# Five row buffers, three sets of statistics and four places for transposes in the first routing of a Macaron block

## The reference

```
x = x + 0.5 * switch_ffn(layernorm(x))     # 8 experts of 1024 hidden units, capacity 512 tokens each
x = x + attention(layernorm(x))            # 16 heads of 16, RMS norm and rotary on q and k
x = x + 0.5 * switch_ffn(layernorm(x))     # the same weights again

# inside switch_ffn, for the 8192 tokens in order:
probs = softmax(x @ w_switch + b_switch);  routes = argmax(probs)
pos   = cumsum(onehot(routes)) * onehot - 1          # place in the expert's queue
keep  = pos < 512;  slot = routes*512 + pos          # those beyond the capacity pass unchanged
y     = relu(buf[slot] @ w1 + b1) @ w2 + b2
```

## Time and profile before

| | |
|---|---|
| median of 3 executions | 2530.02 us (2524.09, 2530.02, 2530.95) |
| profiled execution, its own time | 2523.72 us |
| its span, first to last instruction | 2521.9 us |
| TensorE, busy share of the span | 87% |
| VectorE, ScalarE | 69%, 69% |
| GpSimd | 39% |
| last scatter of the first routing landed | 192.75 us |
| first expert matmul (L619) | 202.92 us |

### The profile page before, as it was taken

How to read it: one execution, slowest core, us unless ns; L and a number is a source line. 1 busy time by engine, 2 the same in 40 slices (tenths; PEclk the granted TensorE clock), 3 DMA queues, 4 the chain that set the end, 5 groups by cost and what they waited for, 6 DMA issues and landing times.

```text
span 2521.9 us, 36418 instructions
## 1 busy us (share of the span) xinstructions
PE 2198.5 (87%) x12974; PEld 1157.5 (46%) x12974; DVE 1738.2 (69%) x2555; ACT 1739.2 (69%) x3390; POOL 977.4 (39%) x1157
## 2 busy tenths in 40 slices
PE   3648994279999989999999998999999999964997
PEld 3547883234434434443443443444344334223986
DVE  2535673467888788887888878888777988302774
ACT  3655666216788778878878877887887887733663
POOL 2554532164056247326515723722651101112542
PEclk9999997658999999999999999999999999755999
DMA  6522530503523334324533332542343422103331
GB/s 244 169 81 101 176 135 25 125 8 85 90 56 86 76 74 86 92 50 86 115 69 83 81 77 57 91 98 56 73 102 61 81 44 32 49 9 126 117 135 59
DMA packets 144901, 218.29 MB, mean 87 GB/s; under 512 B 32224, under 2 KB 100954, under 8 KB 144464
## 3 DMA queue, kind: packets, MB, share of 16 engines
q1 hardware_dynamic: 135504, 199.01, 32.6%
q0 software_dynamic: 9216, 16.95, 1.9%
HBM read 129.59 MB, written 84.80 MB: 85 GB/s over the span
## 4 chain that ended last, share of the span: by engine, by line
PE 75%; DVE 11%; ACT 5%; issue 4%; POOL 2%; DMA 2%; SPq 1%; another core or an unknown queue 0%; POOLq 0%; DVEq 0%; ACTq 0%
PE PS L754 18%; PE PS L738 18%; PE PS L721 10%; PE PS L666 6%; DVE NMX L1265 6%; PE PS L548 4%; PE PS L575 3%; PE PS L698 3%; PE PS L637 2%; PE PS L635 2%; PE PS L636 2%; PE PS L619 2%; PE PS L621 2%; PE PS L620 2%; ACT PB L966 1%
## 5 line engine op out<-in xcount | busy, mean ns | idle before, releaser
L1265 DVE TENSOR_REDUCE NMX<-PS 128x1 f32<-128x1024 f32 x1024 | 1223.4, 1220 | 327.6 <-PE PS L721 303.5
L966 ACT ACTIVATE PB<-PS 128x512 f32<-128x512 f32 x2048 | 1102.4, 603 | 256.6 <-PE PS L738 239.3
L738 PE MATMUL PS<-QF,KF 51*128 51x512 f32 x2048 | 816.6, 472 | 22.9 <-ACT PB L966 13.9
L721 PE MATMUL PS<-KF,QF 49*128 49x512 f32 x2048 | 720.3, 450 | 51.7 <-DVE NMX L1265 37.0
L738 PEld LDWEIGHTS PS<-QF,KF 51*128 51x128 f32 x2048 | 335.2, 189 | 593.2 <-ACT PB L966 309.8
L754 PE MATMUL PS<-PB,V 128*17 128x512 f32 x4096 | 558.3, 618 | 0.2
L721 PEld LDWEIGHTS PS<-KF,QF 49*128 49x128 f32 x2048 | 316.0, 190 | 188.2 <-DVE NMX L1265 118.8
L1363 POOL TENSOR_TENSOR RS<-VE,NEGH 128x8 f32<-128x8 f32 x24 | 40.4, 1682 | 398.8 <-DVE VE L1060 398.7
L1192 DVE TENSOR_TENSOR HLR<-HL,HHR 128x512 fp32r<-128x512 f32 x128 | 88.7, 693 | 92.6 <-ACT HHR L896 92.6
L635 PE MATMUL PS<-W2H,HLR 128*128 128x256 f32 x512 | 143.1, 279 | 0.0
L637 PE MATMUL PS<-W2H,HHR 128*128 128x256 f32 x512 | 141.8, 277 | 0.0
(11 more groups left out here) (168 smaller groups left out, 3328.2 us busy)
## 6 DMA issues: line engine op xcount, KB each, us to landing
W<-in_w SPq DMA_DIRECT2D x32, 1024.0 KB
QF<-qs SPq DMA_DIRECT2D x192, 128.0 KB, 4.8
KF<-qs SPq DMA_DIRECT2D x192, 128.0 KB, 7.2
qs<-HI SPq DMA_DIRECT2D x64, 256.0 KB, 2.1
qs<-R1R SPq DMA_DIRECT2D x64, 256.0 KB, 2.3
buf<-ZT SPq DMA_DIRECT2D x16, 520.0 KB, 9.5
BUF<-buf SPq DMA_DIRECT2D x16, 520.0 KB, 8.4
PX<-x2d SPq DMA_DIRECT2D x8, 1024.0 KB, 5.3
```

What stands on the lines that cost most here:

```text
L721: m = e.matmul(PS[:, 2 * i + half, :], QF[k][at:at + ROWS_S, p * SEQ + ti * 128:p * SEQ + ti * 128 + 128], KF[k][at:at + ROWS_S, p * SEQ + ...
L738: e.matmul(PS[:, bank, :], KF[k][at:at + ROWS_ST, p * SEQ + sbk * 128:p * SEQ + sbk * 128 + 128], QF[k][at:at + ROWS_ST, p * SEQ + th * 51 ...
L966: e.activation(PB[j % 3][:, h * 512:(h + 1) * 512], PS[:, place["e", tile], :], ACT.Exp).then_inc(e_out, 1)
L1265: e.tensor_reduce(NMX[:, u % 2, at:at + 1], PS[:, 2 * i:2 * i + 2, :], AX.XY, ALU.max, negate=True).then_inc(s_max, 1)
```

## The change

Everything the diff does falls into six parts.

1. Buffers. Five row buffers (`xbuf[c % 5]`), load c + 5 in place of c + 4; `ST6`, `MV`, `VE`, `RS`, `NB`, `SM`, `OHB` threefold in the first routing.
2. Transposes. The four groups of a batch get four places, in `XTP` (free in this stage), and the transposes become a generator of their own, `turned`, apart from the logits. A place is free again when the same group's logits of the batch before are done.
3. Offsets. The first routing's come from `FIRST`, later by far: inverse 2, normal 5 to 8, transposes 7 to 10, logits 9 to 12, shift 14, exp 16, softmax 17, one-hot 18, own 20, count 22, slots 23, settle 25 to 28, scatter 27. STRIDE stays 8.
4. Start. Rows of batch 0 first, then `CST`, `WSW`, triangle, ones, `BSW`, rows of batch 1, the zeroing, rows of 2 to 4, then `GQ` (a semaphore of its own). The rotary tables are made at n = 64.
5. Weights. `B1` and expert 0's are loaded after load 6, expert 1's after load 7, `WQKV` and `WP` after store 3. ACT and DVE do expert 0's w1 and w2 splits at n = 64, in the loop.
6. Second routing. The same offsets as before, but transposes of g = 1..3 stand one iteration earlier (48, 49, 50), apart from the logits; the last batch uses the four places of `XTP`.

```
+FIRST = Way(inverse=2, normal=[5 + i // 2 for i in range(8)], transposes=[7 + g for g in range(4)],
+            logits=[9 + g for g in range(4)], shift=14, exp=16, softmax=(17, 17), onehot=(18, 18),
+            own=20, count=22, slots=(23,) * 5, settle=[25 + i // 2 for i in range(8)], scatter=27)
 LEAVE = 43
+LATER = Way(... transposes=[LEAVE + 4 + g for g in range(4)], logits=[LEAVE + 6 + g for g in range(4)], ...)
...
-        xbuf = [QX] + [put(f"NX{i}", [128, 8, ROW]) for i in range(3)]
+        xbuf = [QX] + [put(f"NX{i}", [128, 8, ROW]) for i in range(4)]
+        SM += [put("SM2", [128, 11, 64])]
...
-        def xtq_buf(c, g):
-            return c % 2 if c < NB else g % 2
+        def xtq(c, g):
+            return XTP[:, :, g * 256:(g + 1) * 256] if c < NB or c == 2 * NB - 1 else XTQ[:, g % 2, :, :]
...
             # SP
+            load_x(0)
             e.dma_start(CST[:, :], cst[:, 0:512 + NT]).then_inc(ld_cst, 16)
-            for b in range(min(4, NB)):
-                e.dma_start(xbuf[b][:, :, XC:XC + D], rows(x_in, b)).then_inc(ld_x[b], 16)
             e.dma_start(WSW[:, :, :], wsw.rearrange("(c p) e -> p c e", p=128)).then_inc(ld_par, 16)
+            (TRIF, ONESF -> ld_tri; BSW -> ld_par)
+            load_x(1)
             e.wait_ge(set_z, 1)
             for z in range(zw):
                 zero(0, z)
-            (WQKV, WP, B1 -> ld_big; load_w(0); load_w(1))
+            load_x(2); load_x(3); load_x(4)
+            (GQ three times -> ld_gq)
             for c in range(NB):
                 store_x(c)
-                if c + 4 < NB:
+                if c + 5 < NB:
                     e.wait_ge(st_x[c], 16)
                     for i in range(8):
                         e.wait_ge(scat[i], 16 * (c + 1))
+                    load_x(c + 5)
+                (c == 1: B1, load_w(0); c == 2: load_w(1); c == 3: WQKV, WP)
...
             # ACT; PE has turned and route the same way
+            def turned(c):
+                way = FIRST if c < NB else LATER
+                for g in range(4):
+                    yield way.transposes[g]
+                    e.wait_ge(xtq_full, 4 * c + g + 1)
+                    if 1 <= c < NB or c == 2 * NB - 1:
+                        e.wait_ge(lg_full, 4 * (c - 1) + g + 1)
+                    elif c >= NB and (c > NB or g >= 2):
+                        e.wait_ge(lg_full, 4 * c + g - 1)
+                    e.copy(xtq(c, g), PS[:, xtq_bank(c, g), :].rearrange("p (a n) -> p a n", a=2)).then_inc(xtq_out, 1)
...
-            for n in range(STRIDE * NB + 24):
+            for n in range(STRIDE * NB + FIRST.scatter):
...
                 side.run(n)
+                if n == STRIDE * NB:
+                    split_w1(0)
+                    split_w2(0)
```

More of the change, by code:

```diff
@@ L56 @@
 PROJ_AT = (32, 33, 34, 35, 36, 37, 38, 39)
-XTQ_AT = (47, 48, 49, 50)
-LOGIT_AT = (49, 50, 51, 52)
+Way = namedtuple("Way", "inverse normal transposes logits shift exp softmax onehot own count slots settle scatter")
+FIRST = Way(inverse=2, normal=[5 + i // 2 for i in range(8)], transposes=[7 + g for g in range(4)],
+            logits=[9 + g for g in range(4)], shift=14, exp=16, softmax=(17, 17), onehot=(18, 18),
+            own=20, count=22, slots=(23,) * 5, settle=[25 + i // 2 for i in range(8)], scatter=27)
 LEAVE = 43
+LATER = Way(inverse=LEAVE, normal=[LEAVE + 1 + i // 2 for i in range(8)], transposes=[LEAVE + 4 + g for g in range(4)],
+            logits=[LEAVE + 6 + g for g in range(4)], shift=LEAVE + 10, exp=LEAVE + 11, softmax=(LEAVE + 12, LEAVE + 13),
+            onehot=(LEAVE + 14, LEAVE + 15), own=LEAVE + 16, count=LEAVE + 17,
+            slots=(LEAVE + 18, LEAVE + 19, LEAVE + 20, LEAVE + 20, LEAVE + 21),
+            settle=[LEAVE + 21 + i // 2 for i in range(8)], scatter=LEAVE + 22)
 LAST = LEAVE + 26
@@ L849, in route @@
+                yield way.exp
                 e.wait_ge(rt_sub, c + 1)
-                e.activation(SM[:, k, 2, :], SM[:, k, 1, :], ACT.Exp).then_inc(rt_exp, 1)
-                yield 14 if c < NB else LEAVE + 17
+                e.activation(SM[k][:, 2, :], SM[k][:, 1, :], ACT.Exp).then_inc(rt_exp, 1)
+                yield way.count
                 e.wait_ge(cum_full, c + 1)
-                e.copy(SM[:, k, 5, :], PS[:, cum_bank(c), 0:64]).then_inc(cum_out, 1)
+                e.copy(SM[k][:, 5, :], PS[:, cum_bank(c), 0:64]).then_inc(cum_out, 1)
@@ L904, in pre_x @@
                 if b == 0:
[L905 removed]
+                    yield from normalized([lambda i: PX[:, i, :]] * 2, 0, pn_rs, b, pn_xn, [6 + i // 2 for i in range(8)])
                 for g in range(4):
@@ L1091, in route @@
                 e.tensor_tensor(v(1), v(0), bc(s8(0)), ALU.subtract).then_inc(rt_sub, 1)
-                yield 12 if c < NB else LEAVE + 12
+                yield way.softmax[0]
                 e.wait_ge(rt_exp, c + 1)
@@ L1098, in route @@
                 own.out(e.tensor_tensor(v(3), v(2), bc(s8(2)), ALU.mult))
-                yield 12 if c < NB else LEAVE + 13
+                yield way.softmax[1]
                 own.wait(e)
@@ L1130, in route @@
                 e.wait_ge(cum_out, c + 1)
-                yield 16 if c < NB else LEAVE + 19
+                yield way.slots[1]
                 e.tensor_tensor(v(7), v(5), v(6), ALU.mult)
@@ L1135, in route @@
                 e.tensor_reduce(s8(6), v(7), AX.X, ALU.add)
-                yield 16 if c < NB else LEAVE + 20
+                yield way.slots[2]
                 own.out(e.tensor_tensor(v(0), v(8), v(6), ALU.mult))
@@ L1141, in route @@
                 e.tensor_scalar(t8(0), s8(6), float(CAP), None, ALU.is_ge)
-                yield 16 if c < NB else LEAVE + 20
+                yield way.slots[3]
                 own.out(e.tensor_tensor(t8(1), TOK[:, b * 8:b * 8 + 8], s8(7), ALU.subtract))
@@ L1145, in route @@
                 own.out(e.tensor_tensor(t8(2), t8(1), t8(0), ALU.mult))
-                yield 16 if c < NB else LEAVE + 21
+                yield way.slots[4]
                 own.wait(e)
```

250 lines of the change are left out of this document (130 added, 120 removed).

## The result

| | before | after |
|---|---|---|
| median of 4 executions | 2530.48 us (2524.09 to 2533.04) | 2507.89 us (2503.47 to 2509.86) |
| profiled execution, its own time | 2523.72 us | 2507.65 us |
| its span | 2521.9 us | 2505.8 us |
| last scatter of the first routing landed | 192.75 us | 147.35 us |
| first expert matmul | 202.92 us | 156.73 us |

The ratio is 0.9912 [0.9889, 0.9935]: faster, by 22.6 us. I had forecast 2487, 43.1 us faster, and 2472 to 2503. The sign is right; the size is half, and the time lies outside the range.

A forecast was written before the change was run, and what follows sets the result against it. It took the kernel before to run at a loop of waits through several engines, with POOL the bound after. 39.1 us (first routing) plus 4.0 (last batch) gave 43.1 off 2530.0: 2486.9, say 2487, range 2472 to 2503.

The forecast's parts named there:

- Attention: Batches 8 to 14, transposes 1 to 3 an iteration earlier: cost 0, 0.5 us either way for each of seven routings.
- The prediction's own sign: In attention: the prediction is wrong if attention's length moves by over 5 us.
- The slower rival: In attention, POOL's normalised tiles late for T1, every tile waits, slower than before: 2535 us, chance 0.02.
- First routing: Start to last scatter's landing: landed at 153.6 us against 192.75, a gain of 39.1 us.
- first scatter: In the first routing, behind slots(0), statistics(3) and inverse(3): at 50.2 us, hardly earlier than before.
- the rival: First routing, PE goes to the higher clock: 7 us gained together, time 2480, chance 0.2.
- the loop of ACT and PE: First routing, one batch's transposes, logits, two normalised tiles and last copy: 13.2 to 13.4 us.
- The bound: First routing: POOL becomes the bound, if barely, with a period of 14.0 to 14.2 us, taken as 14.1.
- the buffers: First routing, load c + 5 behind scatters(c): rows there after 17.7 us, wanted after 21.3, cover 3.6 us.
- The splits: w1 and w2 at n = 64: 4.3 us on ACT, 1.9 covered, so L3(7) about 2.5 us late.
- End of the stage: Behind the last scatter of the first routing: moving w2's split out of there is worth nothing.
- Last batch: Second routing's last batch, T1 and T2 ahead of L0 with four places: saves 4 us.

The follow-up runs named there:

- experiment 4: The kernel before with only the new order of transposes and logits in batches 8 to 14 of the second routing: 2555.33 us, ratio 1.0075.
- experiment 9: The changed kernel again, unaltered, timed against the kernel before on one chip: 2506.26 us, ratio 0.99.
- experiment 10: The kernel of experiment 7 again, timed beside the unaltered changed kernel on one chip: 2488.15 us, ratio 0.982 to the kernel before.
- experiment 1: The changed kernel with the old order of transposes and logits in batches 8 to 14: 2487.55 us, ratio 0.9812 to the kernel before.
- experiment 6: Experiment 1 with the first instruction of the inverse issued twice on POOL in the first routing: 2451.18 us in one execution.
- experiment 5: Experiment 1 with four row buffers instead of five, load c + 4: 2483.47 us in one execution.
- experiment 7: Experiment 1 with expert 0's w1 and w2 splits moved behind the loop of the first routing: 2441.43 us in one execution.
- experiment 2: The changed kernel with logits ahead of transposes within each iteration, batches 8 to 14: 2485.05 us, ratio 0.9801 to the kernel before.
- experiment 3: The changed kernel with the logits of batches 8 to 15 one iteration earlier: 2486.43 us, ratio 0.981 to the kernel before.
- experiment 8: The kernel before with the start alone (batch 0's rows first, GQ and rotary tables late): 2467.98 us, ratio 0.9934.

## Why the prediction was right in sign and wrong in size

**The step that failed** is *Attention*: "the same work stands in other iterations ... Cover 10 us, and I take 0, with 0.5 us either way for each of seven." I asked whether the *input* of the earlier transposes would be ready, found 10 us of cover, and closed the step. An operation moved in an in-order queue has three conditions: its input is there, its output has a free place, and what stood around it keeps its order. The second and third I didn't work out. Front and diff had all of it: `lg_full >= 4c + g - 1` is a wait for L(g - 2), and with `turned` begun ahead of `route` T(g) and L(g - 2) fall in the same iteration in that order. In the first routing I had followed each copy to its wait; for attention I only moved iterations. The step cost 27.7 us in one profile, 17 in the other, and some 20 by the timed kernels: experiment 4 gives 19.3, experiments 9 and 10 18.1 (with the splits' place in it). The prediction's own sign, attention's length moving by over 5 us, stood at 34.

**My range for it was too narrow in kind.** I allowed 0.5 us a batch. The stall by itself is 1.3, 9 us for seven, and would have been noticed but would not have broken the range (2487 and 9 is 2496). What broke it is that PE, at 2.4 GHz and full in attention, went on at half the clock after it in four of seven batches, which cost up to 9.2 us in one, with no row in the trace of before at that place. The slower rival had the right mechanism in outline (PE waits in order and every tile of attention behind it) with the wrong trigger (POOL's tiles, where it was ACT's copy) and without the clock, so it got 0.02.

**First routing: 39.1 foretold, 45.4 measured.** The terms: first scatter 44.53 for 50.2; from there to scatters(4) 56.1 for 56.4; the drain to scatters(7) 35.6 for 34.8; last landing behind it 11.1 for 12.2. Nearly all is the first scatter. One part is the clock: experiment 1 had no such stretch (24 logits in 5.13 us at 32.56) and its first scatter is at 47.63, so the rival was worth 3 us where it occurred. I had given it 7 us, and expected it for the whole stage. In the other profiles with this first routing and without the doubled inverse it is 44.3 to 44.5 with such a stretch and 47.4 to 47.6 without. The other part is the loop of ACT and PE: back to back, eight logits take 1.71 us (5.13 / 3) and four transposes 1.0 (2.99 / 3), four times 10.8 us, where I had 11.3 and 0.9 of starts and waits; batch 1's logits in experiment 1 end 11.7 us behind batch 0's, not 13.3.

**The bound and the buffers were right.** POOL is the bound, with 13.7 for 14.1 (experiment 6), and the loop of the buffers has the length I gave it: 24.0 measured for 24.5 with four of them (experiment 5). The cover of the fifth is thin, as the sum said. In the changed kernel the rows of batch 7 are 2.5 us late, and 1.1 of that comes through to POOL.

**The splits** beside the scatters were given 2.5 us on the last logits. What they cost, 0.7 to 1.7 us, comes ahead of scatters(5), by slower instructions of POOL, and behind the loop they would cost 1.1 us at the last scatters (experiment 7).

**End of the stage** was given 0, and is 0.8: 9.4 us from the landing to the first expert matmul for 10.2. With w2's split gone from there, DVE starts on the gathered rows when BUF has landed, 3.85 us behind the last scatter's landing in place of 4.72. I had taken 4.75 us for that load from the second routing; here it takes 3.64.

**Last batch: 4 us**, as foretold: the distance goes from 12.2 to 16.1. No experiment takes it apart; it rests on the trace.

Put together with what was measured, the routing's 46.2 and the last batch's 3.9 would have given 2480. Experiments 1, 2, 3 and 10, where only these act, took 2485 to 2488 on chips where before was 3 to 5 us slower: 45 to 51 us gained.

**Open.** Why the clock falls behind the longer iterations in some batches and not in others was not settled; experiments 1 to 4 show only that without them it does not fall there. Nor was the weak place at the start of each batch looked into. It is the larger one: 245 to 257 us for the seven on the other chips, in the kernel before too, against 223 on the chip of experiments 5 to 8.

## What to carry to other kernels

When an operation is moved in an engine's program, check for it and for whatever it passes not only that the input is ready but that every place it fills, here `XTQ` and the PSUM bank, is freed by something that stands *ahead* of it on the other engine: a wait that used to be satisfied an iteration ago can come to point into the same iteration, behind the producer. Two generators that interleave need an order for the iterations in which both yield, and consumer first is the safe one if they share places. A few tenths of a microsecond of stall beside a full PE should be priced as a chance of the clock falling, not as its own length.

## What the runs showed of the hardware that was not expected

**The busy column hardly shows the stall behind which the clock fell.** In the window 825.30 to 833.00 PE is busy for 7.56 of 7.70 us and behind it the granted clock is 0.50 for 13 us; in experiment 1 it is busy for 7.60 of 7.60 and stays at 1.00. What is lost is overlap and work: L747 and L764 start 0.47 us apart (827.20 and 827.67) where experiment 1's pair starts together (830.48), and the window holds 50 matmuls in place of 62. The Trainium skill (TensorE: Matmul & The Clock Gate, Part 1) says that the gate goes by how busy the array has been of late. The busy column of the trace differs by 2% between the two windows, so it neither bears the rule out here nor speaks against it; no run tells more.

**POOL slows beside DVE's splits.** In the changed kernel, at expert 0's splits:

```profile
107.86 2.50 DVE L1194 TENSOR_TENSOR W10R<-W,W1H 128x512 fp32r<-128x512 f32 x4 [1.77 <-ACT W1H L893]
...
108.51 1.50 POOL L1423 DMA_INDIRECT buf<-NX,IDX  x1 [0.30 <-issue]
...
112.19 0.64 POOL L1548 TENSOR_TENSOR AB<-QX,NB 128x8 f32<-128x8 f32 x1
```

A scatter takes 1.50 us in place of 0.97, and one step of AB 0.64 in place of 0.21, beside DVE operations with two inputs of 128x512 in float32. In experiment 7 the slower scatters move with the splits, to 140 us.

**Chips differ.** The same kernel before took 2490.59 us on one chip and 2530 to 2536 on the others. With the old order, attention took 1642 us on that chip (experiments 5 to 8) and 1675 on the two of experiments 1 and 10, and 32 of the 33 us lie in the first iterations of each batch, where the clock dips on the one and hardly on the other.
